# Constant products behind each norm, and three tiles at once at the start of the linear attentions

## The chip, the cores and the metric

One core of a Trainium2 chip runs the kernel. The metric is the device time of one launch in microseconds. Numbers of the profile come from one profiled execution; L413 is line 413 of the kernel before.

## The reference, cut to what matters

Four layers are applied to one graph of 512 nodes with 768 features: graph attention or graph convolution, a token mixer, and feed-forward networks or experts. Most sublayers start from a layer norm over the 768 features. What this change touches are the norms and the mixers of layers 1, 2 and 3, which are linear attentions with 12 heads of 64:

```python
mu = jnp.mean(x, axis=-1, keepdims=True)
var = jnp.mean(jnp.square(x - mu), axis=-1, keepdims=True)
y = (x - mu) * jax.lax.rsqrt(var + LN_EPS) * ln_gamma + ln_beta
q, k, v = (_elu1(qkv[0]), _elu1(qkv[1]), qkv[2])
kv = jnp.einsum('bhnd,bhne->bhde', k, v)
k_sum = jnp.sum(k, axis=2)
z = 1.0 / (jnp.einsum('bhnd,bhd->bhn', q, k_sum) + EPS)
out = jnp.einsum('bhnd,bhde->bhne', q, kv) * z[..., None]
```

## The kernel before, in words

Activations stay in SBUF, transposed: 128 partitions by 6 chunks of 128 features (KC = 6) by 512 nodes (N). Every large product is done in three matmuls (`mm3`, L412 to L418): high part times high part (L413), and the two mixed products with a low part (L417, L418). Weights come in as blocks of 128 by 768; SyncE loads them, GpSimd splits each into a high and a low part (L361, L364), six blocks in flight, and TensorE hands each back (`blocks_used`). TensorE writes eight PSUM banks; a bank is free again when its reader says so (`use(b)` waits for that, `done` names the reader). Each engine has its own program in order; semaphores tie them together.

**A norm** (TensorE L501 to L520, ScalarE L1173, VectorE L1621): TensorE sums the features with a matrix of ones (L509, bank 6), VectorE subtracts the mean (L1624), ScalarE squares (L1178), TensorE sums the squares (L515, bank 7). Then VectorE scales (L1629), ScalarE takes the root, VectorE the reciprocal (L1632), and chunk by chunk VectorE multiplies, ScalarE makes the high part and VectorE the low part (L1616 or L1619), which is what TensorE waits for. `norm_twice` (L1647) is the same with two outputs, B first, then A. The norm is run nine times in this form: ahead of the MLP of layer 0, the experts of layer 0, the attention of layer 1, the feed-forward of layer 1, the graph convolution of layer 2, the experts of layer 2, the attention and the MLP of layer 3, and the experts of layer 3. The experts begin with a small router product (`router_t`, L811), the feed-forward of layer 1 with a small product (L1014) and then fp32 ones (L1027).

**A linear attention** (TensorE L681, ScalarE L1377, VectorE L2001) is a hardware loop of three iterations, each with two groups g of 128 features. For each group TensorE computes keys and values with nodes on the partitions ("pairs", 256 columns wide, 4 node tiles m by 6 chunks k by 3 matmuls, into banks 3g+1 and 3g+2), and queries transposed (a "tile", 512 columns wide, 6 by 3 matmuls, into bank 3g). VectorE adds the bias rows (L2017, L2018), ScalarE and VectorE make the feature maps (L1382 to L1388, L2024, L2029). Then TensorE multiplies keys by values for both groups (L707) and queries by the results (L713 into bank 3g, L715 into bank 3g+1). The hand-back at the end of an iteration is VectorE's: for g = 0 it copies bank 1 and frees it (L2038), takes a reciprocal (L2039), multiplies bank 0 and frees it (L2040); then the same for g = 1 with banks 4 and 3. The next iteration's first product goes to bank 1, and bank 0 is asked for only by the tile behind the pairs. Only the first iteration of an attention has chunk waits (L694), and in the attentions of layers 1 and 3 they come right behind a norm; the attention of layer 2 uses a norm finished long before. After the loop `turn_t` (L434) starts the projection; it asks for bank 0 first (L441).

Of the kernel before, what the change touches and what calls it, by code (L numbers as in the profile page):

```python
# [30 lines left out]
P = 128  # L31
N = 512
D = 768
KC = D // P
NT = N // P
# [139 lines left out]
def build(nc, t, out, only=None, LOOP_EVENTS={}):  # L175
# [3 lines left out]
    for p in parts:  # L179
        whole, n = p in WHOLE, sum(s[1] for s in stretches)  # L180
# [5 lines left out]
    with ctx:  # L186
# [8 lines left out]
        w_hi = sb("w_hi", [P, 2, 3, KC, P], F32R)  # L195
        w_lo = sb("w_lo", [P, 2, 3, KC, P], F32R)
# [27 lines left out]
        ones_r = sb("ones_r", [P, P], F32R)  # L224
# [44 lines left out]
        ps = ctx.enter_context(nc.psum_tensor("ps", [P, 8, N], F32))  # L269
# [35 lines left out]
        bank_free = {r: [sem(f"bank_free_by_{r}{b}") for b in range(8)] for r in ("act", "dve")}  # L305
        act_to_dve, act_to_pe = sem("act_to_dve"), sem("act_to_pe")
        dve_to_act, dve_to_pe = sem("dve_to_act"), sem("dve_to_pe")
# [68 lines left out]
        def _(pe):  # L376
            S = Side(pe, "pe", None, LOOP_EVENTS)
            S.pending = {}

            def use(b):  # L380

                if S.pending.get(b):
                    reader = S.pending.pop(b)
                    pe.wait_ge(bank_free[reader][b], S.due(bank_free[reader][b]))

            def done(mm, b, reader):
                mm.then_inc(tile_for[reader], 1)
                S.pending[b] = reader

            def blocks(n=1):  # L390
                pe.wait_ge(w_split, S.due(w_split, n))

# [2 lines left out]
            def blocks_used(n=1, last=True):  # L395
                if not last:
                    owed[0] += n
                    return
                pe.matmul(ps[0:2, 7, 0:2], ones_b[:, :], ones_b[:, :], start=True, stop=True,
                          skip_group_check=True).then_inc(w_used, n)  # L400
# [11 lines left out]
            def mm3(o, wh, wl, xh, xl, first, last):  # L412
                mm = pe.matmul(o, wh, xh, start=first, stop=False, skip_group_check=True)  # L413
                if owed[0]:
                    mm.then_inc(w_used, owed[0])
                    owed[0] = 0
                pe.matmul(o, wh, xl, start=False, stop=False, skip_group_check=True)  # L417
                return pe.matmul(o, wl, xh, start=False, stop=last, skip_group_check=True)  # L418

            def tile_t(b, g, j, X, reader, chunks=range(KC), c0=0, c1=N, since=None):  # L420

                use(b)
                for n, k in enumerate(chunks):
                    if since:
                        pe.wait_ge(dve_to_pe, since[k])
                    mm = mm3(ps[:, b, c0:c1], w_hi[:, g, j, k], w_lo[:, g, j, k], X[0][:, k, c0:c1], X[1][:, k, c0:c1],
                             n == 0, n == len(chunks) - 1)
                done(mm, b, reader)

            def chunks_due():  # L430

                return [S.due(dve_to_pe) for k in range(KC)]
# [68 lines left out]
            def norm(since=None):  # L501
                use(6)
                for j in range(KC):
                    if since:
                        pe.wait_ge(dve_to_pe, since[j])
                    elif j in S.pending:

                        pe.wait_ge(bank_free["dve"][j], S.seen.get(bank_free["dve"][j].name, 0) + 1)
                    mm = pe.matmul(ps[:, 6], ones[:, :], norm_src[0][:, j], start=j == 0, stop=j == KC - 1,  # L509
                                   skip_group_check=True)  # L510
                done(mm, 6, "dve")
                use(7)
                for j in range(KC):
                    pe.wait_ge(act_to_pe, S.due(act_to_pe))
                    mm = pe.matmul(ps[:, 7], ones[:, :], aux[:, j % 4], start=j == 0, stop=j == KC - 1,  # L515
                                   skip_group_check=True)
                    if j < 2:
                        mm.then_inc(tile_for["act"], 1)
                done(mm, 7, "dve")
                normed[:] = chunks_due()  # L520

            def norm_twice():
                norm()
# [24 lines left out]
            norm_src, normed = [x], [0] * KC  # L548
# [132 lines left out]
            def linear_attention(X, what):  # L681

                with S.loop(what, 3) as i:
                    for g in range(2):
                        blocks(2)
                        for m in range(NT):
                            b = 3 * g + 1 + m // 2
                            if m % 2 == 0:
                                use(b)
                            c = slice(m * P, m * P + P)  # L690
                            o = ps[:, b, (m % 2) * 256:(m % 2) * 256 + 256].rearrange("p (j c) -> p j c", j=2)
                            for k in range(KC):
                                if g == m == 0:
                                    pe.wait_ge(dve_to_pe, normed[k])  # L694
                                mm = mm3(o, X[0][:, k, c], X[1][:, k, c], w_hi[:, g, 0:2, k], w_lo[:, g, 0:2, k],
                                         k == 0, k == KC - 1)
                            if m % 2 == 1:
                                done(mm, b, "dve")
                        blocks_used(2, False)
                        blocks()  # L700
                        tile_t(3 * g, g, 2, X, "act")
                        blocks_used()
                    for g in range(2):
                        pe.wait_ge(dve_to_pe, S.due(dve_to_pe))
                        use(6 + g)
                        for m in range(NT):
                            mm = pe.matmul(ps[:, 6 + g, 0:P + 2], k_n[:, g, m], v_n[:, g, m], start=m == 0, stop=m == NT - 1,  # L707
                                           skip_group_check=True)
                        done(mm, 6 + g, "dve")
                    for g in range(2):  # L710
                        pe.wait_ge(bank_free["dve"][6 + g], S.coming(bank_free["dve"][6 + g]))
                        use(3 * g)
                        done(pe.matmul(ps[:, 3 * g], kv[:, g], q_t[:, g], start=True, stop=True), 3 * g, "dve")  # L713
                        use(3 * g + 1)
                        done(pe.matmul(ps[:, 3 * g + 1], k_sum[:, g], q_t[:, g], start=True, stop=True), 3 * g + 1, "dve")  # L715
                    S.due(dve_to_pe, 2)
                n = S.seen[dve_to_pe.name]
                return [n - 4] * 4 + [n - 1, n]
# [167 lines left out]
            for e in range(EC):  # L886
                pe.wait_ge(hot_made, e + 1)
                for m in range(NT):
                    mm = pe.matmul(ps[:, m], hot[:, e % 4, 0, m * P:m * P + P], hot[:, e % 4, 1, :], start=e == 0,  # L889
                                   stop=e == EC - 1, skip_group_check=True)  # L890
# [118 lines left out]
            if part("ffn1"):  # L1009
# [8 lines left out]
                for n in range(2):  # L1018
                    for f in range(KC):
                        q = 6 * n + f  # L1020
                        c = slice(0, N if q < 2 else 8)
# [1617 lines left out]
```

## Time and profile before

| | |
|---|---|
| median of 3 runs | 3457.87 us (3457.13 to 3461.19) |
| the profiled execution's own time | 3452.86 us |
| its span | 3451.1 us |
| mean granted TensorE clock | 0.937 of full |
| TensorE matmul busy | 3123.8 us (91%) |
| VectorE busy | 1746.5 us (51%) |
| ScalarE busy | 750.5 us (22%) |
| GpSimd busy | 1421.5 us (41%) |
| chain that ended last | TensorE 83%, VectorE 10%, issue 3%, ScalarE 2%, GpSimd 1% |

The granted clock is a share of 2.4 GHz; 0.50 is the lower of TensorE's two levels, 1.2 GHz. A matmul's listed duration includes the pipeline, so neighbours overlap: the pace of a stream is the distance from one start to the next. In the timeline the bracket behind a row is the idle time of the engine ahead of it and what ended it.

### The profile page before, as it was taken

Reading aid. Unit: us, or ns where it says so; the run is one execution under the profiler, and the core shown is the slowest. Engines: PE = TensorE matmul, PEld = TensorE weight load, DVE = VectorE, ACT = ScalarE, POOL = GpSimd, SP = SyncE. Lnnn points to the kernel's source line nnn. Section 1 sums busy time; section 2 is a strip of 40 time slices with the busy share of each in tenths; the row PEclk is TensorE's granted clock in tenths of the full one; section 3 lists DMA queues with packets and bytes.
Section 4 is the critical chain, followed back from the end, with each engine's and each line's share of the span. In section 5 each row is a group of like instructions: output and inputs, shape, how many; then the busy total and the mean of one; then the engine's idle time right before and its main releaser. Section 6 shows DMA issues by size and latency. Waiting matters only on the chain.

```text
span 3451.1 us, 39618 instructions
## 1 busy us (share of the span) xinstructions
PE 3123.8 (91%) x14183; PEld 2459.9 (71%) x14183; DVE 1746.5 (51%) x2948; ACT 750.5 (22%) x1316; POOL 1421.5 (41%) x1007
## 2 busy tenths in 40 slices
PE   8999798999999968989766879899999998979978
PEld 3576577788888855768545568678888886768858
DVE  7634798466554355347675344543334437641131
ACT  1044111333332212112124112110111113121122
POOL 2021387344344523635300024446666654516500
PEclk9999898999999989999877779999999999989986
DMA  2011365122112211212200122223233322203213
GB/s 78 21 46 35 114 210 178 51 65 70 59 55 69 83 41 52 87 55 87 69 0 9 60 92 64 69 66 101 87 100 96 96 87 70 77 28 100 92 48 109
DMA packets 91268, 256.99 MB, mean 74 GB/s; under 512 B 10335, under 2 KB 10975, under 8 KB 90852
## 3 DMA queue, kind: packets, MB, share of 16 engines
q1 hardware_dynamic: 80352, 219.45, 20.9%
q10 hardware_dynamic: 10788, 35.83, 3.0%
q8 instruction: 81, 1.33, 0.2%
q14 instruction: 47, 0.39, 0.0%
HBM read 253.67 MB, written 1.57 MB: 74 GB/s over the span
## 4 chain that ended last, share of the span: by engine, by line
PE 83%; DVE 10%; issue 3%; ACT 2%; POOL 1%; DMA 0%; DVEq 0%; ACTq 0%; POOLq 0%
PE ps L413 22%; PE ps L417 21%; PE ps L418 21%; PE ps L889 2%; DVE aux L1818 2%; PE ps L515 1%; PE ps L509 1%; PE ps L1124 1%; PE ps L996 1%; PE ps L1027 1%; PE ps L768 1%; PE ps L779 1%; PE ps L761 1%; PE ps L753 1%; DVE hot L2140 1%
## 5 line engine op out<-in xcount | busy, mean ns | idle before, releaser
L361 POOL TENSOR_SCALAR w_hi<-raw 128x768 fp32r<-128x768 f32 x498 | 455.7, 915 | 1805.8 <-PE ps L413 1463.3
L364 POOL TENSOR_TENSOR w_lo<-raw,w_hi 128x768 fp32r<-128x768 f32 x498 | 974.1, 1956 | 41.5
L413 PE MATMUL ps<-H_hi,w_hi 128*128 128x512 f32 x804 | 318.9, 397 | 20.2 <-issue 15.5
L417 PE MATMUL ps<-H_lo,w_hi 128*128 128x512 f32 x804 | 316.5, 394 | 0.0
L418 PE MATMUL ps<-H_hi,w_lo 128*128 128x512 f32 x804 | 316.5, 394 | 0.0
L413 PE MATMUL ps<-B_hi,w_hi 128*128 128x512 f32 x720 | 291.7, 405 | 21.0 <-DVE B_lo L1616 14.9
L413 PE MATMUL ps<-A_hi,w_hi 128*128 128x512 f32 x780 | 307.8, 395 | 1.8 <-DVE sel_now L2062 1.8
L417 PE MATMUL ps<-A_lo,w_hi 128*128 128x512 f32 x780 | 304.7, 391 | 0.0
L418 PE MATMUL ps<-A_hi,w_lo 128*128 128x512 f32 x780 | 304.1, 390 | 0.0
L417 PE MATMUL ps<-B_lo,w_hi 128*128 128x512 f32 x720 | 283.3, 393 | 0.0
L418 PE MATMUL ps<-B_hi,w_lo 128*128 128x512 f32 x720 | 282.7, 393 | 0.0
L1913 DVE TENSOR_TENSOR x<-ps,x 128x512 f32<-128x512 f32 x102 | 70.5, 692 | 273.6 <-PE ps L418 270.1
L413 PEld LDWEIGHTS ps<-H_hi,w_hi 128*128 128x128 f32 x804 | 153.3, 191 | 59.0 <-issue 24.0
L413 PEld LDWEIGHTS ps<-A_hi,w_hi 128*128 128x128 f32 x780 | 146.8, 188 | 46.4 <-issue 13.7
L413 PEld LDWEIGHTS ps<-B_hi,w_hi 128*128 128x128 f32 x720 | 137.0, 190 | 56.3 <-issue 28.7
L417 PEld LDWEIGHTS ps<-H_lo,w_hi 128*128 128x128 f32 x804 | 153.4, 191 | 32.2 <-issue 0.5
L418 PEld LDWEIGHTS ps<-H_hi,w_lo 128*128 128x128 f32 x804 | 153.1, 190 | 32.3
L418 PEld LDWEIGHTS ps<-A_hi,w_lo 128*128 128x128 f32 x780 | 146.9, 188 | 31.0
L417 PEld LDWEIGHTS ps<-A_lo,w_hi 128*128 128x128 f32 x780 | 146.7, 188 | 29.3
L417 PEld LDWEIGHTS ps<-B_lo,w_hi 128*128 128x128 f32 x720 | 136.8, 190 | 31.0 <-issue 4.1
L418 PEld LDWEIGHTS ps<-B_hi,w_lo 128*128 128x128 f32 x720 | 136.7, 190 | 29.2
L413 PE MATMUL ps<-w_hi,H_hi 128*128 128x384 f32 x432 | 147.5, 341 | 2.9 <-ACT aux L1245 2.9
(438 smaller groups left out, 5955.8 us busy)
## 6 DMA issues: line engine op xcount, KB each, us to landing
raw<-stream_dram SPq DMA_DIRECT2D x558, 384.0 KB, 3.0
w_ring<-w_dram ACTq DMA_DIRECT2D x39, 384.0 KB, 3.5
u_rows<-rows_dram ACTq DMA_DIRECT2D x8, 768.0 KB, 6.0
rows<-rows_dram ACTq DMA_DIRECT2D x7, 768.0 KB, 4.1
w_last<-w_dram ACTq DMA_DIRECT2D x9, 384.0 KB, 3.6
x<-x_dram ACTq DMA_DIRECT2D x1, 1536.0 KB, 8.9
out_dram<-x ACTq DMA_DIRECT2D x1, 1536.0 KB, 5.1
orf<-orf_dram ACTq DMA_DIRECT2D x6, 192.0 KB, 3.1
```

Of the source, the lines that this page charges most:

```text
L361: pool.tensor_scalar(w_hi[:, b // 3, b % 3], raw[:, b // 3, b % 3], 1.0, 1.0, ALU.mult, ALU.mult)\
L364: pool.tensor_tensor(w_lo[:, b // 3, b % 3], raw[:, b // 3, b % 3], w_hi[:, b // 3, b % 3], ALU.subtract)\
L413: mm = pe.matmul(o, wh, xh, start=first, stop=False, skip_group_check=True)
L417: pe.matmul(o, wh, xl, start=False, stop=False, skip_group_check=True)
L418: return pe.matmul(o, wl, xh, start=False, stop=last, skip_group_check=True)
L509: mm = pe.matmul(ps[:, 6], ones[:, :], norm_src[0][:, j], start=j == 0, stop=j == KC - 1, skip_group_check=True)
L515: mm = pe.matmul(ps[:, 7], ones[:, :], aux[:, j % 4], start=j == 0, stop=j == KC - 1, skip_group_check=True)
L753: done(pe.matmul(ps[:, b, 0:ORF], k2[:, m * P:m * P + P], w, start=True, stop=True), b, "act")
L761: done(pe.matmul(ps[:, b], w[:, r * P:r * P + P], q2[:, :], start=True, stop=True), b, "act")
L889: mm = pe.matmul(ps[:, m], hot[:, e % 4, 0, m * P:m * P + P], hot[:, e % 4, 1, :], start=e == 0, stop=e == EC - 1, skip_group_check=True)
L1818: ins = dve.tensor_tensor_reduce(flat[:, r * D:r * D + D], w1_slot(n % W1_RING), u_rows[:, h % 2, r], 1.0, 0.0, ALU.mult, ALU.add, u_all[: ...
L1913: ins = dve.tensor_tensor(dst[:, j], ps[:, j], dst[:, j], ALU.add)
```

## The change

TensorE gets a helper that writes n products of the matrix of ones with itself, 512 columns wide, into a bank; if the bank still has a reader, it first waits for that reader. Each of the nine norms ends with 30 of these into bank 0, behind the last sum of squares. In the linear attentions group 0 of each of the three iterations waits for three weight blocks and for banks 0, 1 and 2 ahead of its first product, then does chunk by chunk the pairs of node tiles 0 and 2 and the query tile, and after that the pairs of node tiles 1 and 3. Group 1 keeps its order. The other engines' programs are unchanged.

```diff
+            def keep_busy(b, n):
+
+                if b in S.pending:
+                    reader = S.pending[b]
+                    pe.wait_ge(bank_free[reader][b], S.coming(bank_free[reader][b]))
+                for _ in range(n):
+                    pe.matmul(ps[:, b], ones_r[:, :], ones_r[:, :].unsqueeze(1).to_broadcast([P, NT, P]), start=True, stop=True,
+                              skip_group_check=True)
...
                 done(mm, 7, "dve")
                 normed[:] = chunks_due()
+                keep_busy(0, 30)
...
                 with S.loop(what, 3) as i:
-                    for g in range(2):
-                        blocks(2)
-                        for m in range(NT):
-                            b = 3 * g + 1 + m // 2
-                            if m % 2 == 0:
-                                use(b)
...
-                            for k in range(KC):
-                                if g == m == 0:
-                                    pe.wait_ge(dve_to_pe, normed[k])
...
-                        blocks_used(2, False)
-                        blocks()
-                        tile_t(3 * g, g, 2, X, "act")
-                        blocks_used()
+                    blocks(3)
+                    for b in range(3):
+                        use(b)
+
+                    def pair(m, k):
+                        c = slice(m * P, m * P + P)
+                        o = ps[:, 1 + m // 2, (m % 2) * 256:(m % 2) * 256 + 256].rearrange("p (j c) -> p j c", j=2)
+                        return mm3(o, X[0][:, k, c], X[1][:, k, c], w_hi[:, 0, 0:2, k], w_lo[:, 0, 0:2, k], k == 0, k == KC - 1)
+
+                    for k in range(KC):
+                        pe.wait_ge(dve_to_pe, normed[k])
+                        pair(0, k)
+                        pair(2, k)
+                        mm = mm3(ps[:, 0], w_hi[:, 0, 2, k], w_lo[:, 0, 2, k], X[0][:, k], X[1][:, k], k == 0, k == KC - 1)
+                    done(mm, 0, "act")
+                    for m in (1, 3):
+                        for k in range(KC):
+                            mm = pair(m, k)
+                        done(mm, 1 + m // 2, "dve")
+                    blocks_used(3, False)
+                    blocks(2)
+                    for m in range(NT):
+                        b = 4 + m // 2
...
+                    blocks_used(2, False)
+                    blocks()
+                    tile_t(3, 1, 2, X, "act")
+                    blocks_used()
```

## Rows read from the trace of the kernel before

**Rows 1.** The page's part 1: busy time and share of TensorE

```profile
PE 3123.8 (91%) x14183; PEld 2459.9 (71%) x14183; DVE 1746.5 (51%) x2948; ACT 750.5 (22%) x1316; POOL 1421.5 (41%) x1007
```

**Rows 2.** TensorE's waits: us in total, times, longest

```profile
PE ps L413 <- DVE B_lo L1616: 32.2, 12, 7.4
PE ps L413 <- DVE A_lo L1619: 28.9, 4, 7.2
...
PE ps L1014 <- DVE aux L2307: 10.4, 1, 10.4
```

**Rows 3.** Timeline (start us, us) at layer 0's second norm

```profile
400.78 5.39 PE L515 MATMUL ps<-aux,ones 128*128 128x512 f32 x12 [1.61 <-ACT aux L1178]
...
413.61 0.77 PE L413 MATMUL ps<-B_hi,w_hi 128*128 128x512 f32 x1 [7.44 <-DVE B_lo L1616]
...
418.85 0.39 PE L413 MATMUL ps<-B_hi,w_hi 128*128 128x512 f32 x1
...
423.20 0.39 PE L417 MATMUL ps<-B_lo,w_hi 128*128 128x512 f32 x1
```

**Rows 4.** Windows: length, busy us of PE, PEld, DVE, ACT, POOL; clock; DMA

```profile
413.60:418.50 4.90, 4.89 (x12) 3.84 (x13) 4.90 (x8) 2.53 (x4) 0.00 (x0) 0.50 0.02 3
...
2037.40:2043.40 6.00, 5.92 (x19) 5.95 (x20) 5.87 (x11) 2.52 (x4) 0.00 (x0) 0.50 0.00 0
...
1641.40:1644.50 3.10, 0.00 (x0) 0.00 (x0) 3.01 (x3) 0.00 (x0) 0.00 (x0) 0.95 0.13 52
1644.50:1647.60 3.10, 3.07 (x7) 2.48 (x8) 3.04 (x3) 0.62 (x1) 0.00 (x0) 0.50 0.00 0
```

**Rows 5.** Timeline at the router of layer 0's experts

```profile
1315.09 1.47 DVE L1619 TENSOR_TENSOR A_lo<-acc,A_hi 128x512 fp32r<-128x512 f32 x2
...
1317.03 0.40 PE L413 MATMUL ps<-A_hi,small_hi 128*8 128x512 f32 x1
```

**Rows 6.** Timeline at layer 1's feed-forward: its first two wide products

```profile
1937.30 7.30 PE L1027 MATMUL ps<-acc,raw 128*128 128x512 f32 x12
...
1944.62 5.42 PE L1027 MATMUL ps<-acc,raw 128*128 128x512 f32 x12
```

**Rows 7.** Timeline of the first iteration of layer 1's attention, four engines' answers

```profile
1536.46 0.55 PE L413 MATMUL ps<-w_hi,B_hi 128*128 128x256 f32 x1 [7.44 <-DVE B_lo L1616]
...
1545.25 0.28 PE L413 MATMUL ps<-w_hi,B_hi 128*128 128x256 f32 x1
...
1550.65 0.40 PE L413 MATMUL ps<-B_hi,w_hi 128*128 128x512 f32 x1
...
1554.94 0.39 PE L413 MATMUL ps<-w_hi,B_hi 128*128 128x256 f32 x1
...
1538.22 0.74 DVE L1616 SCALAR_TENSOR_TENSOR B_lo<-acc,cols,B_hi 128x512 fp32r<-128x512 f32 x1
...
1539.54 0.74 DVE L1616 SCALAR_TENSOR_TENSOR B_lo<-acc,cols,B_hi 128x512 fp32r<-128x512 f32 x1
...
1563.88 0.29 DVE L2017 TENSOR_TENSOR aux<-ps,rows 128x128 f32<-128x128 f32 x1 [0.95 <-PE ps L418]
...
1568.09 0.69 ACT L1387 ACTIVATE scr<-ps,cols 128x512 f32<-128x512 f32 x1 [2.45 <-PE ps L418]
```

**Rows 8.** Timeline where that attention's second iteration begins, and GpSimd in the third

```profile
1574.21 1.02 PE L715 MATMUL ps<-q_t,k_sum 128*128 128x512 f32 x2
...
1575.19 0.28 PE L417 MATMUL ps<-w_lo,B_hi 128*128 128x256 f32 x1
...
1577.62 0.69 DVE L2040 TENSOR_TENSOR aux<-ps,row 128x512 f32<-128x512 f32 x1
...
1617.33 0.84 POOL L361 TENSOR_SCALAR w_hi<-raw 128x768 fp32r<-128x768 f32 x1 [11.22 <-PE ps L413]
```

**Rows 9.** Timeline behind that attention's loop: the projection asks for bank 0

```profile
1643.74 0.69 DVE L2040 TENSOR_TENSOR aux<-ps,row 128x512 f32<-128x512 f32 x1
...
1644.53 0.77 PE L413 MATMUL ps<-H_hi,w_hi 128*128 128x512 f32 x1 [3.18 <-issue]
```

More of the change, by code:

```diff
@@ L683, in linear_attention @@
                 with S.loop(what, 3) as i:
-                    for g in range(2):
-                        blocks(2)
-                        for m in range(NT):
-                            b = 3 * g + 1 + m // 2
-                            if m % 2 == 0:
-                                use(b)
-                            c = slice(m * P, m * P + P)
-                            o = ps[:, b, (m % 2) * 256:(m % 2) * 256 + 256].rearrange("p (j c) -> p j c", j=2)
-                            for k in range(KC):
-                                if g == m == 0:
-                                    pe.wait_ge(dve_to_pe, normed[k])
[L695 to L698, printed above, removed]
-                        blocks_used(2, False)
-                        blocks()
-                        tile_t(3 * g, g, 2, X, "act")
-                        blocks_used()
+                    blocks(3)
@@ new lines, in linear_attention @@
+                    done(mm, 0, "act")
[7 more added lines that the diff above has]
+                        b = 4 + m // 2
+                        if m % 2 == 0:
+                            use(b)
+                        c = slice(m * P, m * P + P)
+                        o = ps[:, b, (m % 2) * 256:(m % 2) * 256 + 256].rearrange("p (j c) -> p j c", j=2)
+                        for k in range(KC):
+                            mm = mm3(o, X[0][:, k, c], X[1][:, k, c], w_hi[:, 1, 0:2, k], w_lo[:, 1, 0:2, k],
+                                     k == 0, k == KC - 1)
+                        if m % 2 == 1:
+                            done(mm, b, "dve")
```

## The prediction, made before the change was run

> **What bounds the kernel now.** I read the page first: TensorE is busy 91% of the span [rows 1], so what counts is what TensorE waits for and at which clock it runs. The list of TensorE's waits, next, shows the norms: it stands 7.4 us behind the last sum of squares where the result goes to B, 7.2 us where it goes to A, four times each (the B row also counts eight short waits inside the attentions), and 10.4 us once, in layer 1's feed-forward [rows 2]. That makes the nine norms. The timeline of one shows the wait and what follows: the twelve sums take 5.39 us, the wait 7.44 us, and the next product starts at 413.61 [rows 3]. The windows view gives the clock: behind the wait it is 0.50 for 4.90 us although TensorE is busy all the time [rows 4]. So a norm costs its wait, and then a slow start. Last I read the hand-over from one attention iteration to the next, because the change puts a new wait there.
>
> **Fillers behind the norm.** At the full clock a 512-wide product of this type starts every 0.229 us: 19 steps from 418.85 to 423.20 [rows 3]. The sums ahead run at one per 0.45 us or less, without a pause, and fillers start at their end. Thirty take 30 x 0.229 = 6.9 us, within 7.2 to 7.4: nothing is made late, and 0.3 to 0.6 us stay empty. Bank 0, for which the fillers may wait, was read before the norm's first sum. VectorE's and ScalarE's chain does not wait for them. At the lower clock thirty would take twice that, 13.7 us, and be 6 us late; the sums' pace excludes it.
>
> The Trainium skill has a rule that speaks against the count: TensorE: Matmul & The Clock Gate, section on the back-to-back issue gap, gives about 131 ns per 512-wide product in a sustained stream. By it thirty would last an estimated 3.9 us and leave 3.5 us empty. The trace's 229 ns disagrees, and I go by it.
>
> What a held clock is worth: a stretch that was all TensorE at half clock takes half the time. Layer 0's MLP: 4.90 / 2 = 2.45 us; layer 3's MLP shows the same stretch again, 2.45; layer 2's convolution 6.0 / 2 = 3.0 [rows 4]. VectorE delivers a chunk each 1.32 us [rows 7], TensorE needs 9 x 0.229 = 2.06 us for one, so the faster products find their input. Together **-7.9 us**. It could be 0, if fillers don't hold the clock, and not more.
>
> Routers: they are paced by VectorE. The last low part is there at 1315.09 + 1.47 = 1316.56, the last three products begin at 1317.03 [rows 5]: at most 0.4 us to win. I take **-0.7** for two of three; on the other side their thin stream could let the clock fall again and each expert turn lose a slow start, 2.45 us, so +5 is the other end.
>
> Layer 1's feed-forward: the first twelve wide products take 7.30 us, the next twelve 5.42 [rows 6]: 1.9 us to win. But the wait is 10.4 us [rows 2], the fillers cover 6.9, and 3.5 us remain empty. Between 0 and 1.9, as an empty 3.1 us is followed by the low clock elsewhere [rows 4]: I take the middle, **-1.0**.
>
> **First iteration of the attentions of layers 1 and 3.** Before, chunks feed only node tile 0; behind the last one come 54 narrow products and the tile, and group 1 begins at 1554.94. Narrow ones start every 0.12 us (45 from 1545.25 to 1550.65) [rows 7]. After, a chunk feeds 3 x (0.12 + 0.12 + 0.229) = 1.41 us of work, about the 1.32 us in which it arrives: 1536.46 + 6 x 1.41 = 1544.9, plus 36 x 0.12 = 4.3, so group 1 begins at 1549.2, 5.7 us earlier. Not all of this arrives. VectorE still has its second norm output and waits for the bias rows; what stands between it and the end of the iteration as a wait for TensorE is 0.95 us in front of L2017 and 2.45 us of ScalarE in front of L1387 [rows 7]. These two go: 3.4 us each, -6.8 for the two attentions. In exchange TensorE is now early and idles some 4 us ahead of L707. After an empty 3.1 us the clock is at 0.50 for 3.1 us [rows 4], a loss of 1.55, here on the chain to bank 0. Per attention -3.4 + 1.55, together **-3.7**; ends -6.8 and 0. Layer 2's attention has no chunk waits and wins nothing.
>
> **Second and third iterations, all three attentions.** Here the new order has nothing to win, as all chunks are there, and its waits are new. Before, TensorE goes from L715 (1574.21) straight into the next iteration (1575.19), because bank 1 was freed by L2038, ahead of the reciprocal. Now it first asks for bank 0, which L2040 frees at 1577.62 + 0.69 = 1578.3 [rows 8]. Behind that wait stands everything TensorE has. The price has a twin: the projection behind the loop asks for bank 0 first, and TensorE idles 3.18 us until 0.1 us after L2040's end [rows 9]; this is one of three such rows, one per attention, all with 3.18. I take 3.2 us. The twin also shows the clock: 0.95 in the empty 3.1 us and 0.50 in the 3.1 us of work behind [rows 4], 1.55 us lost. So 4.75 us per iteration, and with two iterations in three attentions 6 x 4.75 = **+28.5 us**. Ends: 6 x 3.2 = 19.2, if the clock stays, and 31. Nothing later absorbs it: the only other waits of an iteration hang on TensorE's own last tile. Costed at nothing: the third weight block asked for early, and blocks handed back later, since GpSimd stands 11.22 us waiting for TensorE in an iteration [rows 8]; if that cover went, a split (about 3 us) would show. SyncE's loads follow GpSimd and have the same cover. The group's number of products is the same.
>
> **Sum.** -7.9 - 0.7 - 1.0 - 3.7 + 28.5 = **+15.2 us**. The profiled execution took 3452.86 us, so 3468.1 by its measure; it lies 5.0 us under the median of the runs shown, and as that is what will be compared I give 3473.
>
> **Rivals.** (1) The stalls come, but the clock survives them, and the wait ahead of L707 too: 19.2 - 7.9 - 0.7 - 1.0 - 6.8 = +2.8 us, 3461. For it: the fall comes only at the end of the empty stretch (0.95 within it). Against: all three twins fall. 14%.
> (2) The change's first half doesn't do what it says: fillers end early or don't hold the clock, and the norms win nothing: 28.5 - 3.7 = +24.8, 3483. For it: there are gaps of 0.3 to 0.6 us left, and products of ones might be something else for the chip than real ones; against: the same instruction and width as the products that hold it everywhere. The skill's 131 ns, above, would lead here. 12%.
> (3) Faster. The wait for bank 0 falls into slack of the loop: if VectorE or ScalarE set the iteration, TensorE could start 3.2 us late and the waits ahead of L707 would shrink by as much. Then -7.9 - 0.7 - 1.0 - 6.8 = -16.4, 3441. It decides from a slack of 3.2 us on that doesn't hang on TensorE. The rows speak against: ScalarE's L1387 had waited 2.45 us for TensorE's last tile, and so moves with it. 5%.
>
> **How the numbers follow.** My own case has 67%; it reads 3473, with 3467 to 3477 around it. The remaining 2% I can't name. A measurement of this kernel can tell about 0.2%, 7 us, from no change. Slower by more than that are my case and rival 2: 78%. Within it is rival 1 with some of the lower edge of mine: 16%. Faster: 6%. The range runs from just under rival 1 to just over rival 2, 3460 to 3484.
>
> **What would show it.** In the changed profile TensorE's first product of the second and third iterations has about 3.2 us idle ahead of it, six times, beside the three of the projections, and the clock at 0.50 behind. The waits of 7.4 us for B_lo shrink to some 0.5 us, and the first products of the MLPs and of layer 2's convolution step at 0.229 us (0.17 us for 384 columns). In the first iteration L707 for group 1 comes some 3 us sooner after the norm. I am wrong if the six idle times are absent, if the clock is 1.00 right behind them, or if it is 0.50 right behind the fillers.

## The result, and the profile after

| | before | after |
|---|---|---|
| median | 3457.5 us (4 runs on the same chip) | 3483.12 us (3480.02 to 3485.44, 4 runs) |
| the profiled execution's own time | 3452.86 us | 3480.02 us |
| its span | 3451.1 us | 3478.2 us |
| mean granted TensorE clock | 0.937 | 0.942 |

The change makes the kernel slower: 1.0076 times the time before, 95% interval 1.0061 to 1.0091. The forecast was 3473 in a range of 3460 to 3484. Span against span it is +27.1 us where the sum said +15.2, so the sign is right and some terms are not. Ratios are to the kernel before on the same chip; experiments ran on different chips, so where two are compared below it is by their ratios or by their traces.

A line of the kernel before between L390 and L520 stands 9 lines further down after the change (L413 is L422), those behind the attention's new body 27 (L707 is L734, L2040 is L2067). The fillers are L396. The page's part 1, which answers to [rows 1]:

```profile
PE 3181.2 (91%) x14444; PEld 2507.7 (72%) x14444; DVE 1746.0 (50%) x2948; ACT 750.3 (22%) x1316; POOL 1420.9 (41%) x1007
```

TensorE is busy 57 us longer. The nine groups of fillers alone are 9 x 7.4 = 67 us; part of that is saved where real products now run at the higher clock. The other engines do what they did. TensorE's waits, which answer to [rows 2] (engine, line waited for: us in total, times, longest):

```profile
PE ps L734 <- DVE q_t L2056: 25.4, 11, 5.0
...
PE ps L422 <- DVE aux L2067: 20.6, 6, 3.5
...
PE ps L422 <- DVE A_lo L1646: 5.5, 16, 0.4
```

Three things are to be seen. The waits of 7 us for the norms' low parts are gone. A wait for L2067, which frees bank 0, stands there exactly six times and takes 3.43 us each. And the wait for `q_t` ahead of L734 has grown to 25.4 us with a longest of 5.0; before, it was 13.2 us, 1.5 at most.

The norm, in the timeline of TensorE (start us, us), answers to [rows 3]:

```profile
405.47 7.41 PE L396 MATMUL ps<-ones_r 128*128 128x512 f32 x30
...
413.48 0.47 PE L422 MATMUL ps<-B_hi,w_hi 128*128 128x512 f32 x1 [0.60 <-DVE B_lo L1643]
```

and the windows of the same place answer to [rows 4] (length, busy us of PE, PEld, DVE, ACT, POOL; clock; DMA):

```profile
405.40:412.80 7.40, 7.40 (x32) 5.63 (x30) 5.74 (x6) 1.61 (x3) 0.00 (x0) 1.00 0.00 1
413.50:418.40 4.90, 4.90 (x22) 4.07 (x23) 4.90 (x8) 2.57 (x4) 0.00 (x0) 1.00 0.01 3
```

Thirty fillers fill the wait up to 0.60 us, and the next 4.9 us hold 22 products at clock 1.00 where [rows 4] has 12 at 0.50.

The handover in layer 1's attention, which answers to [rows 8] (timeline of TensorE, then windows):

```profile
1563.06 2.10 PE L734 MATMUL ps<-v_n,k_n 128*128 128x130 f32 x8 [4.20 <-DVE q_t L2056]
1567.85 2.10 PE L734 MATMUL ps<-v_n,k_n 128*128 128x130 f32 x8 [2.70 <-DVE q_t L2056]
...
1578.29 0.36 PE L422 MATMUL ps<-w_hi,B_hi 128*128 128x256 f32 x1 [3.46 <-DVE aux L2067]
```

```profile
1563.00:1568.00 5.00, 2.25 (x9) 1.96 (x9) 3.94 (x15) 2.80 (x7) 2.42 (x2) 0.50 0.50 147
1568.00:1571.00 3.00, 3.00 (x10) 2.41 (x11) 1.11 (x5) 0.00 (x0) 0.00 (x0) 0.50 0.06 20
...
1579.90:1583.00 3.10, 3.10 (x13) 2.76 (x12) 3.01 (x3) 0.00 (x0) 0.00 (x0) 0.50 0.00 0
```

The wait for bank 0 is there, and some 1.3 us behind its end begins a stretch at half clock; the row above lies within it. That first iteration's L734 also runs at half clock: its eight products take 2.10 us, before they took 1.16. The stretch goes on behind them, and a like one stands at L734 in the second iteration of layer 2's attention:

```profile
1567.85:1572.70 4.85, 4.85 (x12) 3.24 (x13) 1.26 (x5) 0.00 (x0) 0.00 (x0) 0.50 0.06 23
...
2170.20:2173.40 3.20, 3.20 (x8) 1.86 (x8) 0.82 (x4) 0.00 (x0) 1.80 (x1) 0.50 0.43 124
```

**Where the 27.1 us are.** I cut both spans at the start of each norm's sums of squares, and inside an attention at the start of the second group's keys-by-values products (L707 or L734) of each iteration. "First iteration" is from the sums of squares to the first such mark, a "period" from one mark to the next. Layer 2's convolution and its attention are parted at the attention's first product. Differences of one profiled execution each, in us:

| piece | forecast | measured |
|---|---|---|
| layer 0's MLP, layer 2's convolution, layer 3's MLP | -7.9 | -2.89 - 1.55 - 2.32 = -6.8 |
| experts | -0.7 | -0.41 - 0.38 - 1.29 = -2.1 |
| layer 1's feed-forward | -1.0 | -0.1 |
| first iteration of attentions 1, 2, 3 | -1.85, 0, -1.85 | +0.70, -0.19, +1.67 = +2.2 |
| two periods each of attentions 1, 2, 3 (33.06 before) | 9.5 each, +28.5 | +12.4, +11.5, +12.0 = +35.9 |
| behind the loops | 0 | -2.0 |
| sum | +15.2 | +27.1 |

Two rows are off, and they have to be read together. The periods are +7.38 and +5.00 in attention 1, +4.82 and +6.70 in attention 2, +7.04 and +4.98 in attention 3. The two first ones of attentions 1 and 3 hold the half clock behind the first iteration's L734, 2.4 and 2.1 us, which the forecast had in its row on first iterations; the 6.70 holds the one of attention 2, 1.7 us, which it did not have. What is left is 29.8 us for six handovers, 5.0 each, against 28.5. The first iterations with their slow stretch cost 0.70 + 1.67 + 2.4 + 2.1 = 6.8 us where the forecast had -3.7, and that is 10.5 of the 11.9 us between sum and span.

The convolution had won 2.78 us behind its norm and lost 1.2 of them again behind a wait of its own, 8.53 us before and 8.52 after, of which the forecast said nothing. Before, the half clock that sets in during this wait lasted 3.0 us beyond its end, now 5.7:

```profile
2071.22:2074.20 2.98, 2.98 (x9) 2.98 (x10) 1.68 (x3) 2.89 (x7) 0.00 (x0) 0.50 0.00 0
...
2075.57:2081.20 5.63, 5.63 (x18) 5.63 (x19) 3.29 (x6) 4.94 (x11) 0.00 (x0) 0.50 0.00 0
```

The first row is of the kernel before, the second of the changed one. All seven kernels with 30 fillers win 1.5 to 1.8 us from this norm to the attention's mark, no more.

The first iterations have a scatter of their own: in the six kernels that keep the old order they take 46.96 to 47.96 us in attention 1 and 46.78 to 48.25 in attention 3, though VectorE ends its norm at the same distance (30.3 us) in all. In the kernel before, half clock lasts 8.7 us beyond the norm's wait in attention 1, in experiment 3, which changes nothing there, 10.8. A difference of that row to the kernel before holds to some 1.5 us.

### The profile page after: what moved, and what is told of

It is laid out like the page before. It is cut to its first block, busy times and chain, and to the rows that moved or that the text cites. A ratio compares the mean times of both kernels' runs of the same rounds, so it can differ in the third digit from the quotient of the medians.

```text
span 3478.2 us, 40131 instructions
## 1 busy us (share of the span) xinstructions
PE 3181.2 (91%) x14444; PEld 2507.7 (72%) x14444; DVE 1746.0 (50%) x2948; ACT 750.3 (22%) x1316; POOL 1420.9 (41%) x1007
## 4 chain that ended last, share of the span: by engine, by line
PE 80%; DVE 13%; issue 3%; ACT 2%; POOL 1%; DMA 1%; DVEq 0%; ACTq 0%; POOLq 0%
PE ps L422 21%; PE ps L426 20%; PE ps L427 20%; PE ps L916 2%; DVE aux L1845 1%; PE ps L524 1%; PE ps L518 1%; PE ps L1151 1%; PE ps L1023 1%; PE ps L1054 1%; PE ps L795 1%; PE ps L806 1%; PE ps L788 1%; PE ps L780 1%; DVE hot L2167 1%
## 5 line engine op out<-in xcount | busy, mean ns | idle before, releaser
L361 POOL TENSOR_SCALAR w_hi<-raw 128x768 fp32r<-128x768 f32 x498 | 454.6, 913 | 1834.7 <-PE ps L422 1492.9
L422 PE MATMUL ps<-H_hi,w_hi 128*128 128x512 f32 x804 | 318.8, 397 | 20.3 <-issue 15.5
L422 PE MATMUL ps<-A_hi,w_hi 128*128 128x512 f32 x780 | 308.4, 395 | 1.8 <-DVE sel_now L2089 1.8
L422 PE MATMUL ps<-B_hi,w_hi 128*128 128x512 f32 x720 | 291.1, 404 | 7.4 <-issue 6.2
L422 PEld LDWEIGHTS ps<-H_hi,w_hi 128*128 128x128 f32 x804 | 153.2, 191 | 58.9 <-issue 24.1
L422 PEld LDWEIGHTS ps<-A_hi,w_hi 128*128 128x128 f32 x780 | 147.1, 189 | 45.8 <-issue 13.7
L422 PEld LDWEIGHTS ps<-B_hi,w_hi 128*128 128x128 f32 x720 | 136.4, 189 | 40.2 <-issue 14.3
L422 PE MATMUL ps<-w_hi,H_hi 128*128 128x384 f32 x432 | 147.4, 341 | 2.9 <-ACT aux L1272 2.9
```

What stands on the lines that cost most here:

```text
L361: pool.tensor_scalar(w_hi[:, b // 3, b % 3], raw[:, b // 3, b % 3], 1.0, 1.0, ALU.mult, ALU.mult)\
```

## The experiments

Theory S in the expectations: the edits cost what the steps of the prediction say.

**1. The fillers alone**, on the kernel before:

```diff
                 normed[:] = chunks_due()
+                keep_busy(0, 30)
```

> The kernel before with the 30 constant products behind each norm and nothing else. Theory S (the six waits for bank 0 cost what the change loses, the fillers win): about 12 us faster than before, 3445: the stages behind the norms gain what the changed kernel showed there (2.9, 2.8 and 2.3 us at layer 0's MLP, the convolution of layer 2 and the MLP of layer 3, some 0.4 at each router), and the two attentions behind a norm 1.3 us each. Rival C (the fillers themselves cost, by contention or by being late): 3457 or more.

Measured: 3443.51 us, ratio 0.9971 (0.9960 to 0.9981). The three stages behind a norm with wide products give -3.18, -1.53 (2.76 behind the norm, 1.2 lost again behind the convolution's own wait) and -2.32 us, the last stage -1.35, layer 1's feed-forward -0.05. The two attentions behind a norm, of which 1.3 us each were expected, win nothing (+0.96 and +0.03 up to the first mark). So fillers do hold the clock, and they are worth 11 us by themselves. Rival 2 is out.

**2. The new order alone**, the changed kernel without its fillers:

```diff
                 normed[:] = chunks_due()
-                keep_busy(0, 30)
```

> The changed kernel without the 30 constant products: the new order of the attentions alone. Theory S: the loss of the change plus what the fillers won, about 3495. Rival C: less than the changed kernel's 3483, because the costly part is gone.

Measured: 3481.34 us, ratio 1.0080 (1.0066 to 1.0093). This missed. I had expected the changed kernel plus the fillers' 11 us; it is level with the changed kernel. So the two halves aren't independent: beside the new order the fillers' gain is lost again. The marks say where. The first iterations of attentions 1 and 3 take 45.1 us here, 1.85 and 1.7 less than before, while in the changed kernel they take 47.66 and 48.45. That is 5.9 us, and attention 2's second period is another 1.6 longer there. Of the six kernels with the new order, the three in which VectorE is not held up (2, 6, 8) take 44.6 to 45.2 us, the other three (changed, 4, 7) 47.7 to 48.5.

**3. The wait alone**: the order of the kernel before, with bank 0 asked for at the head of each iteration:

```diff
                 with S.loop(what, 3) as i:
+                    use(0)
                     for g in range(2):
```

> The kernel before with one wait added, for bank 0 at the head of each attention iteration; order of products and fillers as before. Theory S: 6 x 4.75 = 28 us slower than before, 3486, with six idle times of 3.2 to 3.5 us. Rival O (the interleaved order of products is what costs, the wait is hidden): 3458, as before.

Measured: 3487.76 us, ratio 1.0092 (1.0077 to 1.0108): one line more than makes up the whole loss. The waits show it as the only new one:

```profile
PE ps L413 <- DVE aux L2041: 20.5, 6, 3.5
```

The six periods are 36.7, 39.4, 38.2, 38.2, 39.2 and 38.2 us against 33.06, together +31.6 us. A wait of the same 3.41 us does not cost the same each time. The timeline and the windows behind the first two:

```profile
1585.95 0.35 PE L413 MATMUL ps<-w_hi,B_hi 128*128 128x256 f32 x1 [3.41 <-DVE aux L2041]
...
1622.65 0.55 PE L413 MATMUL ps<-w_hi,B_hi 128*128 128x256 f32 x1 [3.41 <-DVE aux L2041]
```

```profile
1586.80:1590.00 3.20, 3.20 (x29) 3.20 (x29) 3.17 (x2) 0.00 (x0) 0.00 (x0) 1.00 0.00 0
...
1622.65:1626.00 3.35, 3.35 (x16) 3.35 (x17) 3.32 (x2) 0.52 (x1) 0.00 (x0) 0.50 0.00 0
```

Behind the first the clock stays at 1.00, and the period is 3.6 us longer, nothing but the wait. Behind the second it is at 0.50 from the first product on, for 6.1 us by narrower windows, and the period is 6.3 us longer: 3.4 + 6.1 / 2 = 6.5. Of the other four, three are 5.1 to 5.2 us longer (3.4 + 3.4 / 2 = 5.1) and one 6.2.

**4. The changed kernel, group 0's query product in bank 6** instead of 0, so that bank 0 has been read by ScalarE long before the next iteration asks for it. The wait for bank 6's first reader is now in `use(b)`, and bank 0, whose last reader is ScalarE, is asked for ahead of the loop and at the end of each iteration (the table of semaphore counts per loop changes with it and is left out):

```diff
+                use(0)
                 with S.loop(what, 3) as i:
...
-                        pe.wait_ge(bank_free["dve"][6 + g], S.coming(bank_free["dve"][6 + g]))
-                        use(3 * g)
-                        done(pe.matmul(ps[:, 3 * g], kv[:, g], q_t[:, g], start=True, stop=True), 3 * g, "dve")
+                        if g:
+                            pe.wait_ge(bank_free["dve"][7], S.coming(bank_free["dve"][7]))
+                        b = 3 if g else 6
+                        use(b)
+                        done(pe.matmul(ps[:, b], kv[:, g], q_t[:, g], start=True, stop=True), b, "dve")
...
+                    use(0)
                     S.due(dve_to_pe, 2)
...
-                        freed(dve.tensor_tensor(aux[:, 2 + g], ps[:, 3 * g], row[:, :], ALU.mult), 3 * g)
+                        b = 3 if g else 6
+                        freed(dve.tensor_tensor(aux[:, 2 + g], ps[:, b], row[:, :], ALU.mult), b)
```

> The changed kernel, but in each attention iteration the product of queries by key-value sums of group 0 goes to bank 6 instead of bank 0, so bank 0 is given back early by ScalarE. Theory S: the six waits of 3.4 us and the slow starts behind them go (about 30 us), and so do the three waits of 3.2 us ahead of the projections (about 11 us, the last two chunks come late): 3442. Rival O: 3475, as only the projections gain.

**5. The same edit on the kernel before:**

> The kernel before, order of products as before, no fillers, with only the bank of the query product of group 0 moved from 0 to 6. Theory S: nothing waits for bank 0 in the loop anyway, so only the three projections gain, 3.2 to 3.9 us each: 11 us faster than before, about 3443. Rival (other causes in the other-bank run): no change from before.

Measured: 4 takes 3436.53 us, ratio 0.9951 (0.9938 to 0.9965); 5 takes 3440.09, ratio 0.9957 (0.9945 to 0.9970). In 4 the six waits are gone, and the projection's too; TensorE goes from the last small product into the next iteration, and into the projection behind the loop, without an idle gap:

```profile
1573.92 1.02 PE L745 MATMUL ps<-q_t,k_sum 128*128 128x512 f32 x2
1574.38 0.68 PE L422 MATMUL ps<-w_hi,B_hi 128*128 128x256 f32 x1
...
1639.61 1.02 PE L745 MATMUL ps<-q_t,k_sum 128*128 128x512 f32 x2
1640.07 0.79 PE L422 MATMUL ps<-H_hi,w_hi 128*128 128x512 f32 x1
```

The periods fall to 32.87 us, all but the first of attentions 1 and 3 (34.4 and 34.6), which hold only the half clock behind the first iteration's L734. Against the changed kernel the span is 45.2 us shorter (3433.0 for 3478.2; 43 us by the ratios), of which the six periods are 34 and the stretches behind the three loops 11.5 (attention 2's is 3.9 us shorter). The wait ahead of the projections stood in the kernel before too: 5 wins 15 us by its ratio, 10 to 19 by its interval, where 11 had been expected.

**6. The changed kernel, blocks handed back later.** Experiment 2 had left a question: why do fillers spoil the first iteration? With them TensorE is through group 0 sooner and gives its three blocks back sooner: GpSimd's next split begins 26.1 us behind the start of the sums of squares in the changed kernel, 27.4 to 27.6 in the kernel before and 28.4 to 28.5 in experiment 2. So it falls on VectorE, which still makes the norm's second output. Here the three blocks of group 0 go back only together with the pairs' two of group 1:

```diff
-                    blocks_used(3, False)
                     blocks(2)
...
-                    blocks_used(2, False)
+                    blocks_used(5, False)
```

> The changed kernel, but the weight blocks of group 0 are handed back to GpSimd only together with those of group 1's pairs. Theory G (the fillers and the new order hand blocks back 1.3 us sooner, GpSimd's splits then run beside the second half of norm_twice and slow VectorE there by 4.6 us): VectorE's second norm output takes as long as before, L707 comes 2 to 3 us sooner in the first iterations of layers 1 and 3, about 3477. Rival K (only the clock makes the first iterations slow): as the changed kernel, 3483.

Measured: 3470.95 us, ratio 1.0049 (1.0036 to 1.0063), 9 us under the changed kernel by the ratios and by the spans (3469.0 for 3478.2). The first iterations drop from 47.66 and 48.45 to 45.22 and 44.67. The timelines of VectorE and GpSimd show the cause. The changed kernel:

```profile
1545.56 0.68 DVE L1699 TENSOR_TENSOR acc<-scr,row 128x512 f32<-128x512 f32 x1
1546.16 0.68 DVE L1646 TENSOR_TENSOR A_lo<-acc,A_hi 128x512 fp32r<-128x512 f32 x1
1546.77 1.31 DVE L1699 TENSOR_TENSOR acc<-scr,row 128x512 f32<-128x512 f32 x1
1548.00 2.33 DVE L1646 TENSOR_TENSOR A_lo<-acc,A_hi 128x512 fp32r<-128x512 f32 x1
1550.26 1.31 DVE L1699 TENSOR_TENSOR acc<-scr,row 128x512 f32<-128x512 f32 x1
1551.49 3.57 DVE L1646 TENSOR_TENSOR A_lo<-acc,A_hi 128x512 fp32r<-128x512 f32 x2
...
1546.30 1.24 POOL L361 TENSOR_SCALAR w_hi<-raw 128x768 fp32r<-128x768 f32 x1 [27.50 <-PE ps L422]
1547.62 2.16 POOL L364 TENSOR_TENSOR w_lo<-raw,w_hi 128x768 fp32r<-128x768 f32 x1
1549.75 1.27 POOL L361 TENSOR_SCALAR w_hi<-raw 128x768 fp32r<-128x768 f32 x1
```

and the later handing back:

```profile
1548.43 0.68 DVE L1645 TENSOR_TENSOR A_lo<-acc,A_hi 128x512 fp32r<-128x512 f32 x1
1549.03 0.68 DVE L1698 TENSOR_TENSOR acc<-scr,row 128x512 f32<-128x512 f32 x1
1549.63 1.47 DVE L1645 TENSOR_TENSOR A_lo<-acc,A_hi 128x512 fp32r<-128x512 f32 x2
...
1554.10 0.29 DVE L2043 TENSOR_TENSOR aux<-ps,rows 128x128 f32<-128x128 f32 x1 [1.97 <-DMA rows<-rows_dram]
...
1556.12 0.84 POOL L361 TENSOR_SCALAR w_hi<-raw 128x768 fp32r<-128x768 f32 x1 [36.25 <-PE ps L422]
```

An operation of VectorE with two inputs in SBUF takes 0.68 us alone. Beside GpSimd it ends 0.54 to 0.55 us behind the end of the split that was running: 1548.08 behind 1546.30 + 1.24 = 1547.54, 1550.33 behind 1547.62 + 2.16 = 1549.78, 1551.57 behind 1549.75 + 1.27 = 1551.02. It takes its turn behind the split rather than going at half pace. By the Trainium skill, SBUF — State Buffer, section on who interferes with whom, an instruction of VectorE with two SBUF inputs and one of GpSimd that reads SBUF lock each other out for a whole instruction; these rows agree. The norm's second output ends 34.9 us behind the sums' start, with the later handing back 29.9. In experiment 2 it ends at 30.3. Of the 5 us, the wait for the bias rows takes up 1.6 in attention 1 (1.97 in the row above, 0.35 in the changed kernel); what comes through to L734 is 2.4 us there and 3.8 in attention 3. The edit was worth more than expected, as the periods are shorter too: five by 0.04 to 0.6 us, the second of attention 2 by 2.1, as its half clock at L734 is gone. One row misleads: the projection's wait, 3.18 us as before, is put down to GpSimd:

```profile
1652.10 0.60 PE L422 MATMUL ps<-H_hi,w_hi 128*128 128x512 f32 x1 [3.18 <-POOL w_lo L364]
```

But VectorE's L2066, which frees bank 0, ends at 1652.00, 0.1 us before this product, as its twin did in [rows 9], and experiment 8, which hands back at the same places, has no such row. So this is still the wait for bank 0, and the later handing back delays nothing.

**7. The clock's part of the wait.** The changed kernel with 13 constant products into bank 7 at the end of each iteration, behind the last small product:

```diff
+                    for _ in range(13):
+                        pe.matmul(ps[:, 7], ones_r[:, :], ones_r[:, :].unsqueeze(1).to_broadcast([P, NT, P]), start=True, stop=True,
+                                  skip_group_check=True)
```

> The changed kernel with 13 more constant products at the end of each attention iteration, so that TensorE is busy for 3 us of each wait for bank 0. Theory K (of the 5 us per iteration 3.2 to 3.4 are the wait and the rest the slow clock behind it): nine slow starts go, 1.6 us each: 14 us faster than the changed kernel, about 3469, with periods of 36.3 us between the L707 of neighbouring iterations. Rival (the clock costs nothing there): 3483.

Measured: 3470.59 us, ratio 1.0048 (1.0035 to 1.0061). Four of six periods are 36.5 us, 3.45 over the 33.06: the wait is whole and its slow clock gone. The other two, the first of attentions 1 and 3, are 38.1 and 38.7. In these two the half clock behind the first iteration's L734 is left. The six periods together are 11.4 us shorter than in the changed kernel; 1.7 of it is the stretch at L734 in attention 2, so 9.7 stand against the 9.3 that the forecast gave the clock at these six places (6 x 1.55). The expectation of 14 us for nine slow starts isn't reached: by the ratios it is 9.7, and behind attention 1's loop the kernel is 2.3 us longer than the changed one.

**8. Both mends on the changed kernel**: experiment 4's bank and experiment 6's handing back.

> The other-bank kernel with the late hand-back too. Theories S and G together: 5 to 6 us under the other-bank kernel, about 3431. Rival K: as the other-bank kernel, 3437.

**9. Fillers and bank on the kernel before**, without the new order:

> The kernel before with two edits only: the 30 constant products in each norm, and the query product of the iterations' first tile group in bank 6. The order of the products is that of the kernel before. Theory S (the edits add up, and the new order adds nothing worth having): 10.9 us as the fillers alone gave, plus 15.1 us as the other bank alone gave, so about 3431 us, a ratio of 0.9925, level with the version that has the new order, the other bank and the late handing back (0.9936). Iterations of 30 to 31 us with no wait for bank 0, norms' gaps at full clock. Rival (the new order still earns its 1.85 us in each of two first iterations, once its bank and its handing back are mended): 3435 us or more, slower than that version.

Measured: 8 takes 3433.44 us, ratio 0.9936 (0.9924 to 0.9949); 9 takes 3432.41 us, ratio 0.9932 (0.9918 to 0.9945). They are level, and both beat the kernel before and the changed one. What each half of 9 gave by itself (11 and 15 us) adds up to 26; it gave 24. The iterations of 9 take 33.06 us, not the 30 to 31 that its expectation had. The new order earns next to nothing even with its two faults mended: the whole runs can't tell 8 from 9, and by the traces the three attentions of 8 are together 2.7 us shorter, 1.2 of it in four periods of 32.73 to 32.79 us. The marks of 8 show why: the first iterations of attentions 1 and 3 are 1.7 and 2.2 us shorter than before, and the periods that follow are 2.8 and 1.6 us longer than the second ones (35.57 and 34.40 against 32.73 and 32.79). TensorE gets to L734 early, waits, and does the rest of the iteration at half clock:

```profile
1572.24 2.09 PE L734 MATMUL ps<-v_n,k_n 128*128 128x130 f32 x8 [4.76 <-DVE q_t L2059]
1574.13 1.92 PE L742 MATMUL ps<-q_t,kv 128*128 128x512 f32 x2
1575.84 1.91 PE L744 MATMUL ps<-q_t,k_sum 128*128 128x512 f32 x2
```

In 9 the same products run at full pace:

```profile
1570.54 1.02 PE L726 MATMUL ps<-q_t,kv 128*128 128x512 f32 x2
1571.40 1.02 PE L728 MATMUL ps<-q_t,k_sum 128*128 128x512 f32 x2
```

Experiment 2, read again with this in mind, says the same: -1.85 us up to the mark, and a first period 1.8 us longer than the second (39.88 against 38.05).

**10. Half the fillers**: experiment 1 with 15 in place of 30.

> The kernel before with 15 constant products in each norm in place of 30, so 15 x 0.228 = 3.4 us of work in a gap of 7.9 us, and some 4 us without work after them. Theory S (the clock falls by what TensorE did just before, so that half the fill leaves the norms' tails slow): the products behind the gap of the multilayer-perceptron norms start at a clock of half, and the gain shrinks from 10.9 us to 0 to 4 us, 3450 to 3455 us. Rival (some activity in the gap is enough to hold the clock): the same gain as with 30, about 3443.5 us, a ratio of 0.997.

Measured: 3457.10 us, ratio 1.0003 (0.9994 to 1.0012): the whole gain is gone. The timeline and the windows at layer 0's second norm:

```profile
406.73 3.98 PE L396 MATMUL ps<-ones_r 128*128 128x512 f32 x15
414.73 0.76 PE L422 MATMUL ps<-B_hi,w_hi 128*128 128x512 f32 x1 [4.03 <-DVE B_lo L1626]
```

```profile
410.70:414.70 4.00, 0.00 (x1) 0.00 (x0) 3.84 (x5) 1.39 (x2) 0.00 (x0) 0.84 0.00 0
414.70:419.80 5.10, 5.07 (x12) 4.04 (x13) 5.10 (x8) 2.71 (x4) 0.00 (x0) 0.50 0.01 3
```

Here an empty 4.03 us behind full-clock work costs as much as an empty 7.44: the clock falls in it and stays at 0.50 for the next 5.1 us.

## Why the prediction was right, and where it was not

**Right: the bound and the main mechanism.** The place (bank 0 asked for at the head of the iteration), the number (six), the size of the wait (3.2 forecast from its twin, 3.43 measured) and the half clock behind it are in the trace, and experiment 3 shows that this wait alone gives a loss at least as large as the whole change's. The price per handover was 4.75 us in the sum; in the changed kernel it is 5.0, a wait of 3.43 and 1.5 to 1.7 us of clock, and experiment 7 gives the clock's part by itself.

**Lucky: where the time landed.** 3483.12 is 0.9 us inside the range, at the 3483 of rival 2, whose mechanism experiment 1 rules out: the fillers hold the clock. The six handovers were forecast within 1.3 us; the sum was 11.9 us too low, nearly all of it from the first iterations.

**Right: the norms, but for one thing behind them.** Directly behind the three norms 2.89, 2.78 and 2.32 us were won, together 8.0 where 7.9 was forecast; the fillers leave 0.60 us where 0.3 to 0.6 was said. Not asked was whether the gain would last: 1.2 us of the convolution's went again behind its next wait, so 6.8 are left. Half the fillers won nothing, as experiment 10 shows. The Trainium skill, TensorE: Matmul & The Clock Gate, gives 131 ns for a product in the section on the back-to-back issue gap; that would have led to 7.4 / 0.131, some 56 fillers, as an estimate. By the 0.229 of [rows 3] they would be over 5 us late. The trace's figure was the one to use.

**Right here, but no constant: "4.75 us per iteration".** The sum took 3.2 + 1.55 from one twin and multiplied it. In the changed kernel all six stretches at half clock behind the wait are 3.0 to 3.4 us long, so it fits. In experiment 3 the same wait cost 0.2, 1.7 (three times) and 2.8 to 2.9 us of clock: the six cost 31.6 us, 5.3 each, where the forecast had 28.5 and gave 31 as its end. The one window that was read showed the middle one of three cases.

**Wrong: "These two go: 3.4 us each".** I took TensorE as what VectorE waits for in the first iteration. In experiment 2, where VectorE ends its norm as before, 1.85 and 1.7 us went, not 3.4. (That is against the kernel before; against experiments 3 and 10, which keep the old order and whose first iterations came out longer, it would be 2.7 and 3.1.) VectorE goes through its norm's second output, then waits for the bias rows of a DMA, then works through both groups, and a good part of this doesn't depend on TensorE's tile. And the slow clock of L734 and what follows took these 1.8 us back: net zero against the kernel before, where the sum kept 1.85 per attention. It had the stretch at half clock, once, at the right place (1.55; measured 1.8 and 1.7 in experiment 2, 2.4 and 2.1 in the changed kernel); it had the gain too large, by a factor of two if the kernel before is the measure.

**Wrong: "Costed at nothing: ... blocks handed back later, since GpSimd stands 11.22 us waiting for TensorE".** The cover named was GpSimd's idle time. What was not asked is what else runs while GpSimd works. In the first iteration blocks come back sooner, not later, because the fillers make group 0 faster, and the splits fall on VectorE's norm, which then ends 4.6 us later than before (34.9 for 30.3). This makes the first iterations 2.6 and 3.3 us longer than in experiment 2, which is the gap between experiment 2's -1.85 and -1.7 and the +0.70 and +1.67 of the table. This is the largest miss of the sum. "VectorE's and ScalarE's chain does not wait for them" was true of the fillers and not of what the fillers set off.

**Wrong, but small: layer 1's feed-forward.** The middle between 0 and 1.9 was taken; the lower end was right. The fillers end 3.61 us ahead of the next product, and the first twelve wide products take 7.23 us against 7.30:

```profile
1941.94 2.74 PE L1041 MATMUL ps<-aux,ones 128*128 128x30 f32 x12 [3.61 <-DVE aux L2334]
1944.50 7.23 PE L1054 MATMUL ps<-acc,raw 128*128 128x512 f32 x12
```

The windows of [rows 4] had an empty 3.1 us followed by half clock; an empty 3.5 should have been costed at no gain at all. Experts gained 1.4 us more than forecast, nearly all in the last one. The stage of layer 0's experts varies by 1.8 us among the runs (-0.4 to +1.4), but the last one gains 1.2 to 1.35 in six of the seven kernels with 30 fillers and nothing in the seventh (experiment 7) and in those without, so this gain goes with the fillers.

**What stays open.** The stretch behind attention 1 is 2.45 us shorter in the changed kernel, but 1.9 to 2.2 in experiments 1, 3 and 10 too, which leave its code as it was; so it is scatter of the profiled executions rather than a gain of the change. What decides which of the three prices a stall of 3.41 us pays was not looked into. How much of the 2.7 us that version 8 has over version 9 in the attentions is the new order's can't be told, as first iterations scatter by as much as 1.5 us each.

## What to carry to other kernels

Before an order of work is made to ask for a buffer sooner, look up who frees it last and how long after the previous user; here one bank number decided some 45 us, while the new order itself was worth next to nothing. Fill a wait of TensorE nearly to its end, and look for the next wait behind it: 30 products won 11 us and 15 none, 3.6 us left empty in layer 1's feed-forward won none either, and the convolution's next wait took 1.2 us of 2.8 back. And when an engine gets faster, ask what it sets free for others, and on whose port that work lands.

## What the runs showed of the hardware that was not expected

- The price of one and the same stall varies. 3.41 us of empty TensorE were followed by 0 us at half clock in one iteration and by 6.1 us in the next, in the same run; the period was 3.6 us longer in the one and 6.3 us in the other.
- VectorE's operations with two SBUF inputs, 0.68 us each, took 1.31 and 2.33 us beside GpSimd's splits, each ending 0.54 to 0.55 us behind one of these; the splits got longer too (1.24 us for L361 in place of 0.84). It is the elapsed time of one behind the other, not a lower pace of both.
- A gain in clock can be lost again at the next wait: in the convolution the half clock behind the second wait lasted 3.0 us in the kernel before and 5.7 with the fillers, 1.2 us of the 2.78 won.
- Constant products count for the clock as real ones do: 1.00 was granted through 7.4 us of them, and behind them.
